# A fused decoder layer in fp32 on one NeuronCore: products of ones in short calls, and the calls of the first four periods in a new order

## What is computed

```
x = layernorm(x + mamba2(x))        # 16 heads of 16 channels, state of 64:
    XBC = silu(W_XBC x + b);  cum = cumsum(W_logA x + b)
    Y = (exp(cum_i - cum_j), j <= i) * (C B^T) @ X;  out = ((W_gate x + b) * Y) @ W_out^T + b
x = layernorm(x + cross_attention(x, context of 77 rows, mask))   # 16 heads of 16
x = layernorm(x + relu(x W1 + b1) W2 + b2)                         # hidden width 1024
```

## Time and profile before

| what | us |
|---|---|
| median of 3 runs | 671.2 |
| profiled execution, its own time | 671.81 |
| span of its instructions | 670.1 |
| first call of the loop (`pv(0)`) begins on TensorE at | 94.68 |
| `pv(2)` (s = 5) and `pv(4)` (s = 6) begin at | 129.67 and 164.03 |
| TensorE busy over the span | 632.9 (94%) |
| VectorE, ScalarE, GpSimd busy | 553.6, 455.1, 469.1 |
| mean granted TensorE clock | 0.98 |

### The profile page before, as it was taken

How to read it: one execution, slowest core, us unless ns; L and a number is a source line. 1 busy time by engine, 2 the same in 40 slices (tenths; PEclk the granted TensorE clock), 3 DMA queues, 4 the chain that set the end, 5 groups by cost and what they waited for, 6 DMA issues and landing times.

```text
span 670.1 us, 22057 instructions
## 1 busy us (share of the span) xinstructions
PE 632.9 (94%) x8342; PEld 542.3 (81%) x8342; DVE 553.6 (83%) x1335; ACT 455.1 (68%) x1115; POOL 469.1 (70%) x756
## 2 busy tenths in 40 slices
PE   6989988889999999999999999999999999999897
PEld 4667766668888888888888888888888888899786
DVE  2367778888899898989899898889889898898764
ACT  3967657677778686868678686868678686433332
POOL 1342666667878687787868687787869687879563
PEclk7799998889999999999999999999999999999999
DMA  3422455444344444545345443445345453634201
GB/s 111 175 52 45 119 119 149 118 128 124 97 121 128 128 119 101 127 127 133 110 121 146 110 136 81 129 138 132 101 124 148 104 138 97 158 96 119 48 17 32
DMA packets 86950, 75.54 MB, mean 113 GB/s; under 512 B 44989, under 2 KB 81725, under 8 KB 86845
## 3 DMA queue, kind: packets, MB, share of 16 engines
q1 hardware_dynamic: 86429, 73.85, 41.2%
q10 hardware_dynamic: 416, 0.28, 0.1%
HBM read 41.53 MB, written 31.72 MB: 109 GB/s over the span
## 4 chain that ended last, share of the span: by engine, by line
PE 74%; DVE 12%; ACT 6%; issue 3%; DMA 2%; POOL 1%; SPq 1%; ACTq 0%; POOLq 0%; DVEq 0%
PE bank L520 12%; PE bank L532 11%; PE bank L365 9%; PE bank L309 5%; PE bank L426 4%; PE bank L499 4%; PE bank L468 4%; PE bank L379 3%; PE bank L509 2%; PE bank L486 2%; PE bank L293 2%; PE bank L352 2%; PE bank L321 2%; PE bank L540 2%; PE bank L393 2%
## 5 line engine op out<-in xcount | busy, mean ns | idle before, releaser
L1115 DVE TENSOR_TENSOR E<-bank,E 128x512 f32<-128x512 f32 x128 | 81.8, 680 | 21.2 <-PE bank L365 17.5
L1503 POOL TENSOR_TENSOR P<-P,rc 128x308 f32<-128x308 f32 x120 | 80.8, 700 | 21.0 <-DVE rc L1276 20.9
L1463 POOL TENSOR_SCALAR_AFFINE_SELECT E<-E 128x508 f32<-128x508 f32 x128 | 80.3, 651 | 0.0
L365 PE MATMUL bank<-Cc,Bc 64*128 64x128 f32 x1024 | 72.6, 287 | 3.7 <-DVE cmat L1098 2.7
L818 ACT ACTIVATE E<-bank 128x512 f32<-128x512 f32 x128 | 68.0, 599 | 10.9 <-PE bank L352 10.6
L365 PEld LDWEIGHTS bank<-Cc,Bc 64*128 64x128 f32 x1024 | 63.2, 192 | 14.4 <-issue 5.6
L532 PE MATMUL bank<-w2h,hh 128*128 128x256 f32 x256 | 74.5, 291 | 0.0
L1527 POOL TENSOR_TENSOR hl<-hr,hh 128x512 fp32r<-128x512 f32 x56 | 72.1, 1297 | 0.3
L532 PE MATMUL bank<-w2l,hh 128*128 128x256 f32 x256 | 71.7, 280 | 0.0
L532 PE MATMUL bank<-w2h,hl 128*128 128x256 f32 x256 | 71.7, 280 | 0.0
L897 ACT ACTIVATE hr<-bank,cst 128x256 f32<-128x256 f32 x128 | 54.7, 495 | 18.6 <-PE bank L520 16.7
(11 more groups left out here) (126 smaller groups left out, 1795.5 us busy)
## 6 DMA issues: line engine op xcount, KB each, us to landing
turn_p<-TP SPq DMA_DIRECT2D x120, 160.0 KB, 2.8
PT<-turn_p SPq DMA_DIRECT2D x30, 640.0 KB, 4.2
xr<-in_x SPq DMA_DIRECT2D x32, 128.0 KB, 2.5
out<-res SPq DMA_DIRECT2D x32, 128.0 KB, 2.8
xT<-in_xT SPq DMA_DIRECT2D x15, 256.0 KB, 3.1
turn_x<-xr SPq DMA_DIRECT2D x120, 32.0 KB, 1.8
tT<-turn_x SPq DMA_DIRECT2D x30, 128.0 KB, 2.7
turn_x<-x SPq DMA_DIRECT2D x120, 32.0 KB, 2.0
```

The costliest lines, as they stand in the source:

```text
L365: i = eng.matmul(b_g[n, u, r][:, 128 * q:128 * q + 128], Bc[k, g % 2, 2 * q + u, cols(n)], Cc[k, g % 2, 2 * q + u, cols(n)], start=True, s ...
L1115: eng.tensor_tensor(E[:, h % 4, r, :, :], b_g[n, u, r][:, :].rearrange("p (h t) -> p h t", h=4), E[:, h % 4, r, :, :], ALU.mult).then_inc( ...
L1463: eng.affine_select(out=E[:, h % 4, r, :, 0:127], in_=E[:, h % 4, r, :, 0:127], compare_op=ALU.is_ge, fill=0.0, base=0, pattern=[[0, 4], [ ...
L1503: eng.tensor_tensor(v, v, rc[:, n % 2, 4 * j:4 * j + 4].unsqueeze(2).to_broadcast([128, 4, S]), ALU.mult).then_inc(p_norm, 1)
```

## The change

1. `warm` issues 14 products when k is 0, and 4 otherwise. There are now sixteen calls in place of six: `warm(0)` and `warm(1)` stand together at the start, and `warm(2)` to `warm(15)` are spread over the prologue. That is 74 products in place of 48.
2. The prologue calls of TensorE, ScalarE, VectorE, GpSimd and SyncE stand in a new order. The same calls are made, and the loop and the epilogue are as before.
3. `x1_turn` and `x2_turn`, which only the last two tiles have, wait for one more semaphore value each.

```
@@ PE @@
             def warm(k):
...
-                for _ in range(8):
+                for _ in range(14 if k == 0 else 4):
...
+                pe.wait_ge(x1_flip, n)
...
+                pe.wait_ge(x2_flip, n)
...
             warm(0)
+            warm(1)
             tok(0)
             tok(1)
+            warm(2)
             cum(0)
+            cum(1)
             bc(0, 0)
-            cum(1)
+            tok(2)
             bc(0, 1)
-            tok(2)
+            ecum(1)
+            warm(3)
             diff(0, 0)
-            ecum(1)
-            warm(1)
...
@@ ACT @@
             cum_top(0)
+            cum_top(1)
             bc(0, 0)
-            cum_top(1)
+            tok(2)
             bc(0, 1)
-            tok(2)
             ecum(1)
             exp_diff(0, 0)
             exp_diff(0, 1)
+            cum_top(2)
             exp_diff(1, 0)
             exp_diff(1, 1)
-            cum_top(2)
+            ecum(2)
             bc(1, 0)
             tok(3)
...
@@ POOL @@
             decay(0, 0)
             decay(0, 1)
+            split_w(0)
             x_resid(0)
...
+            x_resid(2)
             decay(2, 0)
...
@@ SP @@
             start()
+            start_kv()
             rows(0)
-            start_kv()
+            load_resid(0)
+            load_w(0)
             rows(1)
-            load_resid(0)
             start_weights()
-            load_w(0)
-            rows(2)
+            load_w(1)
             load_x(2)
             load_resid(1)
+            load_w(2)
+            rows(2)
             put_x1(0)
             get_x1(0)
+            load_x(3)
+            rows(3)
             load_resid(2)
...
```

More of the change, by code:

```diff
@@ L566, in _ @@
             warm(0)
+            warm(1)
             tok(0)
             tok(1)
+            warm(2)
             cum(0)
+            cum(1)
             bc(0, 0)
[L571 removed]
+            tok(2)
             bc(0, 1)
[L573 removed]
+            ecum(1)
+            warm(3)
             diff(0, 0)
[L575 to L576 removed]
             diff(0, 1)
+            warm(4)
+            warm(5)
             gmat(0, 0)
+            gmat(0, 1)
+            warm(6)
             diff(1, 0)
+            cum(2)
             diff(1, 1)
[L581 to L582 removed]
             state_in(0)
+            y(0)
             bc(1, 0)
[L585 removed]
+            ecum(2)
             gate(0)
+            gmat(1, 0)
+            warm(7)
             out_proj(0)
             tok(3)
+            state_turn(0)
+            gmat(1, 1)
+            state_in(1)
+            cum(3)
             bc(1, 1)
[L590 to L591 removed]
+            warm(8)
+            warm(9)
+            inter(1)
+            ecum(3)
             keys()
[L593 removed]
             tok(4)
[L595 to L601 removed]
+            y(1)
+            gate(1)
+            bc(2, 0)
+            state_turn(1)
+            values()
+            diff(2, 0)
+            cum(4)
             diff(2, 1)
[L603 to L605 removed]
+            diff(3, 0)
+            out_proj(1)
             query(0)
[L607 to L612, removed]
             inter(2)
[L614 removed]
             gmat(2, 0)
@@ L617, in _ @@
             gmat(2, 1)
-            tok(5)
[L619 to L622, removed]
+            state_in(2)
+            state_turn(2)
+            warm(10)
+            score(0)
+            gate(2)
+            ecum(4)
+            warm(11)
+            y(2)
+            warm(12)
+            diff(4, 0)
+            warm(13)
+            gmat(3, 0)
+            tok(5)
+            out_proj(2)
+            bc(2, 1)
+            gmat(3, 1)
+            cum(5)
+            tok(6)
+            state_in(3)
             query(1)
-            bc(2, 1)
+            warm(14)
             score(1)
[L626 to L633, removed]
             diff(4, 1)
-            gmat(3, 1)
+            gmat(4, 0)
             state_turn(3)
-            tok(6)
+            y(3)
             inter(3)
-            y(3)
             gate(3)
-            gmat(4, 0)
+            warm(15)
+            cum(6)
+            out_proj(3)
             bc(3, 0)
-            out_proj(3)
-            cum(6)
             inter(4)
```

182 lines of the change are left out of this document (92 added, 90 removed).

## The result

The changed kernel takes 677.5 us (median of 12 runs, 674.36 to 680.91), the kernel before 672.53 (12 runs beside them, 670.6 to 676.6). The ratio is 1.0065, with a 95% interval of 1.004 to 1.009: 0.65% slower, some 4.4 us. The forecast was 2.5 us slower. The ratio came out the same on a second occasion, 1.0062 (1.0032 to 1.0093), so the loss is small but real.

A forecast was written before the change was run, and what follows sets the result against it. The loop was taken as TensorE-bound and unchanged, the prologue as near that bound; added products, 8.7 us of waits and SyncE's queue put diff(5, 0) 3.5 us later, less 1.0 for overlap: +2.5 us, 673.7 us, range 664.5 to 680.

The forecast's parts named there:

- The start: From the first products to exp_diff(0, 0): 0.7 us earlier, between 0 and 1.6, through a higher clock.
- The price for the context loads: At the start, loads issued earlier on SyncE could delay ScalarE's constants by 0 to 1.3 us; taken as 0.
- The mark after it: In the prologue, diff(0, 0) ends near 22.1 us; without any wait after it pv(0) would start at 88.3 us.
- The waits: TensorE's waits for banks and other engines in the new prologue order: together 8.7 us, with pv(0) ready at 97.0.
- The queue: At the prologue's end on SyncE, rows(5) comes behind nine stack_v DMAs and lands 1.2 us after TensorE is ready.
- The rival in which SyncE's queue decides: If x1_blocks(2) comes later than about 81 us, each microsecond delays diff(5, 0); over 678 us, chance 0.17.
- No wait there leads to it: In s = 5 on GpSimd, split_w(3) leaves (3.4 us) but no wait leads to it; taken as 0.
- What I took back: From the +3.5 us at diff(5, 0), 1.0 us taken off for overlap of the waits, leaving +2.5 us.
- The step from `diff(5, 0)` to the end: From diff(5, 0) through s = 4 and s = 5: a microsecond later there is a microsecond later at the end.
- The signs named beforehand: Trace marks in prologue and loop that would show the forecast right, such as diff(5, 0) between 97 and 100 us.
- The products: In the prologue behind the start, 48 products of 0.26 us in place of 32: 4.2 us more TensorE time, net of the start.
- A reading: Of the earlier trace's page: the granted clock is full from slice ten on; no size given.

The follow-up runs named there:

- the second profile: The changed kernel run once more, unchanged, as a reference for later runs: 1.0062 of the kernel before; its profiled execution took 677.0 us.
- the slowest execution: The profiled execution of the changed kernel, slowest of its twelve: 680.91 us.
- the old order with its queue mended, the run with `stack_v` early: The kernel before with the four stack_v calls together where stack_v(0) stands: 669.31 us, 0.9935 of the kernel before.
- the new one with its queue mended: The changed kernel with the four stack_v calls behind rows(4) and decay(5, 1) directly behind decay(5, 0): 675.71 us, 1.0046 of the kernel before.
- absent with `stack_v` early: The changed kernel with the four stack_v calls together behind rows(4) on SyncE: 675.74 us, 1.0024 of the kernel before.

## Why the prediction was right

The direction, the size (2.5 forecast, 4.4 measured) and the place were right; the forecast was too small by 1.9 us. Step by step:

- **The start.** Forecast: full clock at `tok(0)`, silus of `bc(0, 0)` at 14.7, `bc(0, 1)` at 17.6 and its silus at 19.8, `exp_diff(0, 0)` at 24.3. Measured: full clock, 14.46, 17.64, 19.72 and 24.34. The reason held as well: the bound is ScalarE, and `bc(0, 1)` waits 2.53 us for the banks of `bc(0, 0)`. About half of the 0.64 us gained at `exp_diff(0, 0)` is chance: ScalarE's first silu began 0.31 us earlier in this execution. The price for the context loads had a slip (987 KB at 349 GB/s take 2.8 us, not 2.7), which changes nothing, since they cost nothing here: VectorE's wait for the constants ended at 6.73, 6.83 before.
- **The mark after it.** Forecast: `diff(0, 0)` ends near 22.1. Both `diff` of tile 0 ran from 22.09 to 22.89. But I let the clock come back there, and it came back near 27: the eight products at 22.82 took 3.78 us in place of 2.06, and the two `gmat` 2.58 in place of about 2.2. That is 2.1 us, the largest error of the walk for this profile, in which `diff(5, 0)` starts 4.1 us later than the 99.2 forecast. In the profile of the more usual execution it starts 1.9 us later than forecast.
- **The waits.** Forecast 8.7 us up to `pv(0)`, measured 9.0. For banks of `bc(1, 0)` 1.1 was forecast, 1.6 measured (1.43 and 0.17); `bc(2, 0)` 0.7, 0.98; `state_turn(2)` 0.7, 0.89; `bc(2, 1)` 1.6, 1.24; `tok(6)` 0.9, 0.92; `inter(3)` 1.3, and 1.6 with its two neighbours. The 0.3 for `diff(3, 1)` didn't show. Two more were wrong and offset each other: `diff(3, 0)` was to wait 2.1 us for `rows(3)` and did not wait (issued 55.23 to 57.84, and read in the group of four products that begins at 58.88, because TensorE itself came some 3.5 us later than the 55.4 of the walk), and `gmat(4, 1)` waits 1.73 us for `out_proj(3)`'s bank, which I had not seen. So that the sum of the waits came within 0.3 us is in part luck; six of its eight terms were there, at 6.3 us forecast and 7.2 measured.
- **The queue.** Forecast: `stack_v` no longer ends last, `rows(5)` does, 1.2 us. Measured 1.04, and 0.78 in the second profile. (The walk took the landing behind the issue as 1.8, 1.5 and 1.6 us at three places; that moves it by 0.3 us at most.) The rival in which SyncE's queue decides was halfway true in the slowest execution: `x1_blocks(2)` came at 83.4, later than the 81 that it named, and `rows(5)` did end last. But TensorE was late as well, so the queue cost 1.04 us there, not the four that the rival gives it. What the queue is worth in the new order stays open between a quarter and two thirds of the loss (1.0046, 1.0024). That it isn't all of it is shown by the old order with its queue mended, which is 6.4 us faster than the new one with its queue mended.
- **The term that was missing.** "No wait there leads to it" was said of GpSimd in s = 4 and s = 5. It holds for `split_w(3)`, but the list also put `decay(5, 1)` behind `soft_norm(2)`, and that is a wait of 1.73 us in the profile after and 2.67 in the second one. What it costs isn't shown (1.0049 without the wait, 1.0062 with it; the intervals overlap).
- **What I took back.** The 1.0 us off for overlap was wrong: the waits did come with their full length. Without it the forecast is +3.5 us, nearer to the 4.4 measured. The step from `diff(5, 0)` to the end, a microsecond for a microsecond, held: 5.45 us there and 5.2 at the end in the second profile.
- **The signs named beforehand.** The full clock at `tok(0)`, `exp_diff(0, 0)` between 24 and 24.5, `rows(3)` after 53, `rows(5)` behind `stack_v` and the same work in the same time from s = 6 on came true. Three did not: TensorE didn't idle ahead of `diff(3, 0)`, the silus of `bc(1, 0)` were at 36.63 and not near 34 (34.40 in the second profile), and `diff(5, 0)` started at 103.30 (101.14 in the second profile), not between 97 and 100.
- **The products.** I priced them at their length, 4.2 us net, with the clock's effect only at the start. The runs say that a price by length is wrong for the early ones: fourteen calls at one product each are slower by 0.65%, not faster. Part of them filled waits (4.6 of 10.9 us), and the clock took the rest and more. For the late ones (`warm(10)` to `warm(15)`) the runs show neither cost nor gain: 1.0023 without 18 of them, between 1.0046 (group before) and 1.0016 with them.
- **A reading.** The slices of the earlier trace rows show nines from the tenth on, which is 90% or more and not a full clock; the earlier trace rows have 0.95 up to 164 us. No term hangs on it.

The low-clock time explains most of the spread of the changed kernel. Over its twelve runs the time rises with the low-clock time, which is 2 x (1 - mean clock) x span: 674.36 us at 9.4 us of it, 680.91 at 27.2, a slope of 0.29 (standard error 0.04) us for each. It would be up to 0.5 if TensorE were the bound in all of that time. For the kernel before, the same reckoning explains little (35 executions of the second group, a slope of 0.11, standard error 0.04, and a fifth of the spread). There the mean clock can't be trusted, since the column can miss the low stretch at the start, as in the run with `stack_v` early.

What is shown is that the new order with its products is some 6 us longer than the old one when the queue is mended in both. What stays open is how that splits. Sixteen more products behind the start are 4.2 us of TensorE's work, and its waits up to `pv(0)` are 9.0 us, against 4.4 without the one for `stack_v` in the old order: 4.6 more. The two together are more than the 5.5 to 6.4 us measured; no run separates them, and none takes the waits away one by one.

## What to carry to other kernels

Look at every queue, SyncE's too, for the last thing ahead of the place where the pipeline begins: the kernel before waited there for 2.5 us for twelve small DMAs, and moving them forward in the queue gave 0.65% without touching anything else, while a new order of five engines gave nothing. Mend it in both kernels before comparing them: here it hid some 2 us of what the new order costs. In this order, written by hand, the waits came with their full length, so a walk through banks, queues and the lists of the other engines finds most of the sum before a run. Products of ones that fill a wait cost nothing, and those that hold the clock are worth what real work follows at the higher clock. Don't weigh them by their length: here 42 fewer made the kernel 0.65% slower.

## What the runs showed of the hardware

- The clock's low stretches come at other places in each execution of the same kernel. In the profiled executions of the kernels that start with 18 products, the stretch behind the projections at low clock was 10.2 us long after the change, 6.8 in the changed kernel once more, and absent with `stack_v` early. The last of these is chance, since nothing differs between them before 61 us. The Trainium skill (TensorE: Matmul & The Clock Gate, Part 1: The HAM clock gate) says that where the transition falls varies from run to run; these runs agree. The page's 500 ns are for the first rise of the clock; the later low stretch differs by up to 10 us here. Over the twelve executions after the change, low-clock time differs by 17.8 us, which at 0.29 is some 5 of the 6.5 us between the fastest and the slowest.
- A product of 128x512 takes 0.45 us at the start of the kernel and 0.26 us at the high level (3.63 and 2.06 for eight). Of the 18 after the change, nine fall between 5.0 and 7.8 us, 0.31 each: the clock rose in their course. The granted clock reads 1.00 from the first microsecond on, so for that stretch the products' own lengths are the better witness. The same holds further on where no change of the clock is on record yet: in the old order with `stack_v` early it reads 1.00 from 8 to 28 us, while `bc(0, 0)` takes 2.09 us, and in the profile of before, at a column of 0.50, the same 2.09.
